# Products without use in TensorE's pauses: a one-core attention and expert kernel

## Chip, core and metric

The kernel runs on one core of one Trainium2 chip. The metric is the device time of one launch in microseconds (us). The kernel before takes 1171.12 us, the median of three runs (1170.22 to 1174.72). About half a per cent, some 5.9 us, is what a measurement of this kernel can tell from no change.

## What is computed

Four sublayers follow each other, each with a layer norm ahead of it, and a layer norm and an addition to x behind it:

```python
x = L0_attn_x                                              # (4, 512, 256)
x = x + _layernorm(_L0_attn_ref(_layernorm(x, axis=-1), ...), axis=-1)
x = x + _layernorm(_L0_ffn_ref(_layernorm(x, axis=-1), ...), axis=-1)
x = x + _layernorm(_L1_attn_ref(_layernorm(x, axis=-1), ...), axis=-1)
x = x + _layernorm(_L1_ffn_ref(_layernorm(x, axis=-1), ...), axis=-1)
```

Attention 0 has an RMS norm, 16 heads of 16, rotary embedding, a causal softmax, an output projection and a residual. The first feed-forward layer sends each token to 2 of 8 experts (256 to 1024 to 256), with at most 640 slots per expert. Attention 1 is a plain causal attention with 16 heads. The last layer computes all of 8 small gated experts and a shared one for every token, and mixes them by top-2 weights.

## The kernel before

The program is a row of blocks, and every engine waits for all others between two of them: setup, a first norm, attention 0 (`attention_phase` with `rope`), the experts (`expert_phase`), attention 1 (`attention_phase` without `rope`), the dense experts (`dense_phase`). Within a block the engines run their own instruction lists in order and meet by semaphores.

An attention handles 4 batches of 512 tokens. Its steady part is a loop over 16 steps (batch and group of four heads) and 11 places in each: TensorE (PE) computes scores for the row maxima into three PSUM banks `ps_a`, scores again into `ps_b`, products with the values into `ps_pv`, and at fixed places one "fill" of the two `ps_m` banks (`fill`: transposes, projections, outputs, routing). Ahead of the loop stand the fills of `FIRST`: the transposes of batch 0 (`yt`), its projections (`pr`) and values (`v`). They wait for `y_first`, the four normalised rows that VectorE (DVE) writes, and for the weights (`weights_in`).

Behind the loop stand the fills of `FINAL`, in the order in which TensorE does them:

```python
final = [("ot", last, 0), ("ot", last, 1), ("out", last, 0), ("out", last, 1)]
...
    final += [("rk", 2, 0), ("rt", last, 0), ("rt", last, 1), ("lg", last, 0), ("rk", last, 0)]
```

The second line is of attention 0 alone. `ot` and `out` are the last batch's output (L884, L901). `rk` counts for each token how many earlier ones chose its expert (two small bf16 matmuls, L869 and L871); `rt` and `lg` are the router's transposes and logits (L884, L862). DVE works through its own list there: it takes `out`, computes the statistics, and then, ahead of the normalisation of the last batch, turns the ranks of batch 2 into slots:

```python
variance(0, b)
if rope:
    place(2)                 # waits for ("rk", 2, 0) of TensorE
for i in range(TPB):
    ln_normalise(b, i)
```

After that come `ln_add`, the statistics of x, `route_rows` (what the transposes `rt` of the last batch wait for), `choose_top`, `count`, and `place` of the last batch. GpSimd (POOL) scatters the rows of batch 2 and of batch 3 to the experts' slots (L535) and waits until all have landed; then the block ends, its semaphores are cleared (L269), and the expert block loads its first rows.

Of the kernel before, what the change touches and what calls it, by code (L numbers as in the profile page):

```python
# [17 lines left out]
P = 128  # L18
BATCH, SEQ, D = 4, 512, 256
# [8 lines left out]
STEPS = BATCH * GROUPS  # L28
# [113 lines left out]
MAXES, PROBS = 11, 10  # L142
# [6 lines left out]
def need(eng, sem, count):  # L149

    if count > 0:
        eng.wait_ge(sem, count)
# [22 lines left out]
def prob_at(T, s):  # L175

    t, k = (T - 1, s - LAG) if s >= LAG else (T - 2, s - LAG + MAXES)
    return (t, k) if 0 <= t < STEPS and k < PROBS else None
# [74 lines left out]
def attention_phase(nc, keep, w, layer, route, w1=None, wide=None):  # L253

    wide = wide or []
    rope = layer == 0
# [9 lines left out]
    ident, identb, mask_q, minus_half = keep["ident"], keep["identb"], keep["mask_q"], keep["minus_half"]  # L266
    FILL, FIRST, FINAL, FILLS_AT, DONE_AT = misc_plan(rope, Q_TILES)
    held_sems = []
    with ExitStack() as ctx:  # L269
# [3 lines left out]
        def psum(name, shape, dt=F32):  # L273
            return ctx.enter_context(nc.psum_tensor(f"a{layer}_{name}", shape, dt))

        def sem(name):
            held_sems.append(nc.alloc_semaphore(name=f"a{layer}_{name}"))
            return held_sems[-1]
# [26 lines left out]
        ps_a = [psum(f"ps_a{i}", [P, SEQ]) for i in range(A_BANKS)]  # L305
# [4 lines left out]
        weights_in, cleared_rows, ones_in = sem("weights_in"), sem("cleared_rows"), sem("ones_in")  # L310
# [7 lines left out]
        a_full, a_free, b_full, exps = sem("a_full"), sem("a_free"), sem("b_full"), sem("exps")  # L318
# [49 lines left out]
        def emptied(eng, name):  # L368
            eng.wait_ge(m_free[FILL[name][0]], FILL[name][1] + 1)
# [412 lines left out]
        def _(pe):  # L782
# [4 lines left out]
            def max_unit(t, k):  # L787

                n = t * MAXES + k
                ps = ps_a[n % A_BANKS]  # L790
                need(pe, a_free, n - A_BANKS + 1)
                for h, i, at in max_work(k):
                    wd = (i + 1) * P
                    last = nc.tensor.matmul(ps[:, at:at + wd], q_st[t % STACKS][:, h // PER_TILE, i * P:wd],  # L794
                                            k_st[t % STACKS][:, h, 0:wd], start=True, stop=(k < 8),
                                            skip_group_check=True)
                    if k >= 8:
                        last = mask(ps, at + i * P)
                last.then_inc(a_full, 1)

            def prob_unit(t, k):

                n = t * PROBS + k
                ps = ps_b[n % B_BANKS]
                need(pe, exps, n - B_BANKS + 1)
                if k == 0 or (k == 2 and Q_TILES == 2):
                    emptied(pe, ("nm", t, k // 2))
                for h, j, at in prob_work(k):
                    wd = SEQ - j * P
                    last = nc.tensor.matmul(ps[:, at:at + wd], k_st[t % STACKS][:, h, j * P:(j + 1) * P],  # L810
                                            q_less[:, h // PER_TILE, j * P:SEQ], start=True, stop=True,
                                            skip_group_check=True)
                last.then_inc(b_full, 1)
# [14 lines left out]
            def pv(t, j):  # L828
                b, g = divmod(t, GROUPS)
                for h in range(HPG):  # L830
                    at = j * P
                    rhs = {0: probs[:, h, :], 1: probs[:, 4 + h, 0:3 * P], 3: probs[:, 4 + h, 3 * P:SEQ],
                           2: probs[:, 8 + h // 2, (h % 2) * 2 * P:(h % 2) * 2 * P + 2 * P]}[j]
                    last = nc.tensor.matmul(ps_pv[h * VW:(h + 1) * VW, at:SEQ], v[:, b % 2, j, g * HPG + h, :], rhs,  # L834
                                            start=(j == 0), stop=(j == 2), skip_group_check=True)
                return last
# [68 lines left out]
                    if half == 1:  # L905
                        last.then_inc(full, 1)

            pe.wait_ge(weights_in, 16 * (10 if rope else 3))
            def fill_whole(name):
                fill(name, 0)  # L910
                if name[0] in HALVED:
                    fill(name, 1)

            for name in FIRST:
                fill_whole(name)
            pe.wait_ge(identr_ready, 1)
            for T in range(STEPS + 2):
                for s in range(MAXES):
                    if T < STEPS:
                        if s == 0:  # L920
                            if T < STACKS:
                                pe.wait_ge(ones_in, (T + 1) * HPG)
                            pe.wait_ge(stacked[T % STACKS], 16 * 2 * HPG * (T // STACKS + 1))
                        max_unit(T, s)
                    if prob_at(T, s):
                        prob_unit(*prob_at(T, s))
                    for name, half in FILLS_AT.get((T, s), ()):
                        fill(name, half)
                    if s == 2 and 0 <= T - 2 < STEPS:
                        pe.wait_ge(masked, (T - 2) * 4 + 3)  # L930
                        pv(T - 2, 1)
                        pv(T - 2, 3).then_inc(pv_done, 1)
                    if s == 5 and 0 <= T - 2 < STEPS:
                        pe.wait_ge(masked, (T - 2) * 4 + 4)
                        pv(T - 2, 2).then_inc(pv_done, 1)
                    if s == 9 and 0 <= T - 1 < STEPS:
                        if (T - 1) % GROUPS == 0:
                            emptied(pe, ("v", (T - 1) // GROUPS, 0))
                            emptied(pe, ("v", (T - 1) // GROUPS, 1))
                        pe.wait_ge(masked, (T - 1) * 4 + 1)  # L940
                        need(pe, pv_copied, T - 1)
                        pv(T - 1, 0).then_inc(pv_done, 1)
            for name in FINAL:
                fill_whole(name)

        @block.vector
        def _(dve):
# [1122 lines left out]
def program(nc, io, out):  # L2070
    with ExitStack() as ctx:
        keep = keep_all(nc, ctx)
        scratch = [nc.dram_tensor(f"scratch{i}", (2, n, 3, P, SEQ), F32, kind="Internal").ap() for i, n in enumerate((2, 4))]
        dispatched = nc.dram_tensor("dispatched", ((E0 + 1) * CAP, D), F32, kind="Internal").ap()
        results = nc.dram_tensor("results", (SLOTS, D), F32, kind="Internal").ap()
        keep["cleared"] = ctx.enter_context(nc.semaphore("cleared"))
        keep["x_loaded"] = [ctx.enter_context(nc.semaphore(f"x_loaded{b}")) for b in range(BATCH)]
        setup_phase(nc, keep, io["x"])
        norm_phase(nc, keep)
        route = {"gates": ctx.enter_context(nc.sbuf_tensor("gates", [P, 2, TILES], F32)),  # L2080
                 "get_at": ctx.enter_context(nc.sbuf_tensor("get_at", [P, 2, TILES], U32))}
        with ExitStack() as moe:
            w1 = {part: moe.enter_context(nc.sbuf_tensor(f"w1_{part}", [P, KC, FF], F32 if part == "raw" else F32R))
                  for part in ("raw", "hi", "lo")}
            experts = {n[3:]: a for n, a in io.items() if n.startswith("m0_")} | {"dispatched": dispatched,
                                                                                 "results": results}
            attention_phase(nc, keep, {n[3:]: a for n, a in io.items() if n.startswith("a0_")} | experts
                            | {"scratch": scratch[0]}, 0, route, w1)
            w2 = {part: moe.enter_context(nc.sbuf_tensor(f"w2_{part}", [P, FC, D], F32 if part == "raw" else F32R))
                  for part in ("raw", "hi", "lo")}  # L2090
            expert_phase(nc, keep, experts, w1, w2)

        wide = [(io[f"m1_{n}"], *(ctx.enter_context(nc.sbuf_tensor(f"w_{n}_{part}", [P, KC, HB * H1], F32R))
                                  for part in ("hi", "lo"))) for n in ("gate", "up")]
        attention_phase(nc, keep, {n[3:]: a for n, a in io.items() if n.startswith("a1_")}
                        | {"scratch": scratch[1], "results": results}, 1, route, None, wide)
        dense_phase(nc, keep, {n[3:]: a for n, a in io.items() if n.startswith("m1_")}, wide, out)
# [41 lines left out]
```

## Time and profile before

| what | value |
|---|---|
| time, median of 3 runs | 1171.12 us (1170.22 to 1174.72) |
| time of the profiled execution | 1182.48 us |
| its span, first to last instruction | 1179.3 us |
| mean granted TensorE clock | 0.906 of full speed |
| PE busy | 975.2 us (83%) |
| DVE, POOL, ACT busy | 620.9, 464.2, 446.0 us |

The profiled execution is 11.4 us longer than the median of the others, and 3.2 us of it lie outside the span. PE is TensorE's matmuls, PEld its weight loads, ACT is ScalarE, SP the engine that issues most DMAs. PEclk is the share of full clock that TensorE was granted: 1.00 is 2.4 GHz and 0.50 is 1.2 GHz. Blocks lie in the span roughly so: attention 0 from 10 to 338 us, experts from 342 to 608, attention 1 from 608 to 952, dense experts from 956 to the end.

### The profile page before, as it was taken

What the parts mean: (1) busy time and instruction counts of PE and PEld (TensorE: products, weight loads), DVE (VectorE), ACT (ScalarE), POOL (GpSimd) and SP (SyncE); (2) the same over time, 40 slices, a digit from 0 to 9 for tenths busy, and PEclk for the clock granted to TensorE, in tenths of its full rate; (3) what the DMA queues carried; (4) which work ended last, traced back from release to release, by engine and by line L of the source; (5) the groups of instructions that cost most, each with busy time, mean ns of one, the idle gap of its engine ahead of it and who ended that gap; (6) DMA issues with size and microseconds to landing.
All of it is one profiled execution on the core that took longest, in us unless ns stands there. A gap on an engine that the chain in (4) does not pass through costs nothing. (4 is left out here: it accounts for less than half of the span.)

```text
span 1179.3 us, 17823 instructions
## 1 busy us (share of the span) xinstructions
PE 975.2 (83%) x6250; PEld 773.6 (66%) x6250; DVE 620.9 (53%) x1802; ACT 446.0 (38%) x800; POOL 464.2 (39%) x432
## 2 busy tenths in 40 slices
PE   3699999887419999999943489899999739999996
PEld 1466767564319999999941256575666427888885
DVE  5666787956513333333335767776666143353534
ACT  0155555443003333333300045555556314433332
POOL 3453544464523333222345243454243415434232
PEclk9799999897659999999985689999999659999998
DMA  3442212010142323332022552423310010000001
GB/s 129 160 149 95 81 54 92 26 50 10 63 173 95 112 90 111 116 115 94 22 83 69 187 170 77 160 87 112 126 55 28 1 46 1 1 2 18 18 1 36
DMA packets 50023, 91.78 MB, mean 78 GB/s; under 512 B 7328, under 2 KB 22944, under 8 KB 49824
## 3 DMA queue, kind: packets, MB, share of 16 engines
q1 hardware_dynamic: 46880, 82.49, 20.8%
q0 software_dynamic: 3072, 8.39, 2.2%
q8 instruction: 39, 0.64, 0.2%
q14 instruction: 32, 0.26, 0.1%
HBM read 54.55 MB, written 36.31 MB: 77 GB/s over the span
## 5 line engine op out<-in xcount | busy, mean ns | idle before, releaser
L746 ACT ACTIVATE a_probs<-a_ps_b 128x512 f32<-128x512 f32 x320 | 188.1, 600 | 190.2 <-PE a_ps_b L810 186.4
L794 PE MATMUL a_ps_a<-a_k_st,a_q_st 128*128 128x256 f32 (+3 forms) x512 | 204.2, 440 | 26.9 <-DMA a_k_st<-scratch 17.3
L1004 DVE CUSTOM_DVE_ANT_0 a_masked_s<-a_ps_a,a_mask_f 128x512 f32<-128x512 f32 (+1 forms) x256 | 155.2, 621 | 86.6 <-PE a_ps_a L794 80.6
L794 PEld LDWEIGHTS a_ps_a<-a_k_st,a_q_st 128*128 128x128 f32 x512 | 102.5, 203 | 89.6 <-issue 42.6
L475 POOL TENSOR_SCALAR_AFFINE_SELECT a_probs<-a_probs 128x512 f32<-128x512 f32 x128 | 80.9, 646 | 198.3 <-ACT a_probs L746 198.0
L1594 POOL TENSOR_TENSOR w_lo<-w_raw,w_hi 128x2048 fp32r<-128x2048 f32 x16 | 73.9, 4616 | 186.7 <-ACT w_hi L1612 186.7
L810 PE MATMUL a_ps_b<-a_q_less,a_k_st 128*128 128x384 f32 (+3 forms) x512 | 140.2, 337 | 3.0 <-ACT a_probs L746 2.1
L810 PEld LDWEIGHTS a_ps_b<-a_q_less,a_k_st 128*128 128x128 f32 x512 | 91.3, 197 | 28.6 <-ACT a_probs L746 17.8
L1620 ACT ACTIVATE exp_h_hi<-exp_ps_u 128x320 fp32r<-128x320 f32 x128 | 49.2, 437 | 148.4 <-PE exp_ps_u L1684 148.4
L834 PE MATMUL a_ps_pv<-a_probs,a_v 128*32 128x512 f32 (+3 forms) x1024 | 94.9, 470 | 10.7 <-POOL a_probs L475 10.7
L1649 DVE SCALAR_TENSOR_TENSOR exp_h_lo<-exp_ps_u,exp_h_hi 128x320 fp32r<-128x320 f32 x128 | 56.8, 485 | 69.5 <-ACT exp_h_hi L1620 69.5
L1799 POOL TENSOR_TENSOR dense_h_lo<-dense_mixed,dense_h_hi 128x512 fp32r<-128x512 f32 x40 | 52.1, 1303 | 104.1 <-ACT dense_h_hi L1852 104.1
L1699 PE MATMUL exp_ps_o<-w_hi,exp_h_hi 128*128 128x256 f32 x320 | 91.2, 285 | 0.0
L1699 PE MATMUL exp_ps_o<-w_hi,exp_h_lo 128*128 128x256 f32 x320 | 90.5, 283 | 0.0
L1699 PE MATMUL exp_ps_o<-w_lo,exp_h_hi 128*128 128x256 f32 x320 | 90.5, 283 | 0.0
L1011 DVE TENSOR_REDUCE a_nmax<-a_ps_a 128x2 f32<-128x512 f32 (+1 forms) x96 | 65.9, 687 | 40.5 <-PE a_ps_a L784 38.4
L884 PE MATMUL a_ps_m<-kept_ident,kept_sub 128*128 128x128 f32 x160 | 30.5, 333 | 65.2 <-DVE kept_sub L950 33.9
L2038 DVE TENSOR_TENSOR dense_product<-dense_gated,dense_ps_u 128x512 f32<-128x512 f32 x40 | 27.5, 687 | 87.1 <-PE dense_ps_u L1869 81.3
L891 PE MATMUL a_ps_m<-a_y_t,a_w_qk 128*128 128x512 f32 x128 | 69.6, 645 | 3.0 <-ACT a_y_t L648 1.9
L884 PEld LDWEIGHTS a_ps_m<-kept_ident,kept_sub 128*128 128x128 f32 x160 | 24.4, 175 | 68.6 <-issue 48.4
L1659 DVE COPY exp_out<-exp_ps_o 128x512 f32<-128x512 f32 (+1 forms) x24 | 14.5, 603 | 97.9 <-PE exp_ps_o L1699 97.9
L1684 PE MATMUL exp_ps_u<-exp_x_t_hi,w_hi 128*128 128x320 f32 x256 | 60.3, 317 | 3.1 <-DVE exp_h_lo L1649 1.9
(238 smaller groups left out, 2296.2 us busy)
## 6 DMA issues: line engine op xcount, KB each, us to landing
w_raw<-in_m_w SPq DMA_DIRECT2D x16, 1024.0 KB, 5.1
scratch<-a_hi SPq DMA_DIRECT2D x24, 512.0 KB, 2.8
scratch<-a_lo SPq DMA_DIRECT2D x24, 256.0 KB, 3.1
a_q_st<-scratch SPq DMA_DIRECT2D x64, 96.0 KB, 2.6
a_k_st<-scratch SPq DMA_DIRECT2D x64, 96.0 KB, 2.6
exp_rows<-dispatched SPq DMA_DIRECT2D x9, 640.0 KB, 4.2
results<-exp_out SPq DMA_DIRECT2D x8, 640.0 KB, 3.0
dispatched<-kept_sub SPq DMA_DIRECT2D x9, 512.0 KB, 2.9
```

Source lines behind the costliest of these rows:

```text
L475: nc.gpsimd.affine_select(out=blocks, in_=blocks, compare_op=ALU.is_ge, fill=0.0, base=0, pattern=[[0, HPG], [1, P]], channel_multiplier=- ...
L746: nc.scalar.activation(probs[:, k, :], ps_b[k % B_BANKS][:, :], ACT.Exp, scale=scale).then_inc(exps, 1)
L794: last = nc.tensor.matmul(ps[:, at:at + wd], q_st[t % STACKS][:, h // PER_TILE, i * P:wd], k_st[t % STACKS][:, h, 0:wd], start=True, stop= ...
L810: last = nc.tensor.matmul(ps[:, at:at + wd], k_st[t % STACKS][:, h, j * P:(j + 1) * P], q_less[:, h // PER_TILE, j * P:SEQ], start=True, s ...
L834: last = nc.tensor.matmul(ps_pv[h * VW:(h + 1) * VW, at:SEQ], v[:, b % 2, j, g * HPG + h, :], rhs, start=(j == 0), stop=(j == 2), skip_gro ...
L891: last = nc.tensor.matmul(ps[:, :], w_qk[:, half, n, :], y_t[:, half, :], start=(half == 0), stop=(half == 1))
L1004: nc.vector.tensor_tensor_reduce(masked_s[n % 2][:, 0:wd], ps[:, 0:wd], mask_f[:, SEQ - wd:SEQ], -1.0, -NEG, ALU.add, ALU.min, nmax[:, t % ...
L1011: nc.vector.tensor_reduce(out, src, AX_X, ALU.max, negate=True).then_inc(a_free, 1)
L1594: nc.gpsimd.tensor_tensor(of["lo"][:, :, :], of["raw"][:, :, :], of["hi"][:, :, :].bitcast(F32), ALU.subtract).then_inc(ready, 1)
L1649: nc.vector.scalar_tensor_tensor(h[1][:, f, cols], ps_u[n % U_BANKS][:, 0:HALF], 0.0, h[0][:, f, cols].bitcast(F32), ALU.max, ALU.subtract ...
L1684: last = nc.tensor.matmul(ps_u[(2 * f + half) % U_BANKS][:, 0:HALF], (w1["hi"], w1["lo"])[i][:, c, f * P:(f + 1) * P], x_t[j][:, c * CAP + ...
L1699: last = nc.tensor.matmul(bank[:, t % 2 * D:(t % 2 + 1) * D], h[i][:, f, t * P:(t + 1) * P], (w2["hi"], w2["lo"])[j][:, f, :], start=(f == ...
```

## The change

TensorE is given products that nothing reads. Each multiplies the bf16 identity by itself, repeated to 512 columns, into the bank `ps_a[0]`. There are 12 ahead of the first transposes of attention 0 and 90 ahead of those of attention 1, both ahead of TensorE's wait for the weights; 36 behind the last `out` fill of each attention; and 60 behind the last `rk` fill of attention 0. Ahead of `FINAL` a wait for the last of DVE's row maxima is added, since the products overwrite a bank that they read. In all 12 + 36 + 60 + 90 + 36 = 234 products.

```diff
-            pe.wait_ge(weights_in, 16 * (10 if rope else 3))
             def fill_whole(name):
                 fill(name, 0)
                 if name[0] in HALVED:
                     fill(name, 1)
 
+            def idle_products(count):
+
+                for _ in range(count):
+                    nc.tensor.matmul(ps_a[0][:, :], identb[:, :], identb[:, :].unsqueeze(1).to_broadcast([P, SEQ // P, P]),
+                                     start=True, stop=True, skip_group_check=True)
+
+            idle_products(12 if rope else 90)
+            pe.wait_ge(weights_in, 16 * (10 if rope else 3))
             for name in FIRST:
                 fill_whole(name)
...
+            pe.wait_ge(a_free, STEPS * MAXES)
             for name in FINAL:
                 fill_whole(name)
+                if name == ("out", BATCH - 1, 1):
+                    idle_products(36)
+                if name == ("rk", BATCH - 1, 0):
+                    idle_products(60)
```

TensorE's instructions at the end of attention 0 in the kernel before, from the last batch's output transposes (L884) to the block's end (L269); `a_hot_sum` and `a_prior` are the operands of an `rk` fill:

```order
L884 MATMUL a_ps_m<-kept_ident,kept_sub 128x128 x8
L901 MATMUL a_ps_m<-a_w_o,a_o_t 128x256 x8
L869 MATMUL a_ps_m<-a_hot_sum,a_before 128x32
L871 MATMUL a_ps_m<-a_prior,a_ones 128x32
L884 MATMUL a_ps_m<-kept_ident,kept_sub 128x128 x8
L862 MATMUL a_ps_m<-a_w_g,a_ry_t 128x8 x8
L869 MATMUL a_ps_m<-a_hot_sum,a_before 128x32
L871 MATMUL a_ps_m<-a_prior,a_ones 128x32
L269 UNCONDITIONAL_BRANCH
```

The same place in the changed kernel:

```order
L884 MATMUL a_ps_m<-kept_ident,kept_sub 128x128 x8
L901 MATMUL a_ps_m<-a_w_o,a_o_t 128x256 x8
L916 MATMUL a_ps_a<-kept_identb 128x512 x36
L869 MATMUL a_ps_m<-a_hot_sum,a_before 128x32
L871 MATMUL a_ps_m<-a_prior,a_ones 128x32
L884 MATMUL a_ps_m<-kept_ident,kept_sub 128x128 x8
L862 MATMUL a_ps_m<-a_w_g,a_ry_t 128x8 x8
L869 MATMUL a_ps_m<-a_hot_sum,a_before 128x32
L871 MATMUL a_ps_m<-a_prior,a_ones 128x32
L916 MATMUL a_ps_a<-kept_identb 128x512 x60
L269 UNCONDITIONAL_BRANCH
```

The numbers at a row's end count matmuls as the program issues them; in the trace an f32 matmul that is not a transpose shows as two instructions. The 36 stand between the last `out` and the ranks of batch 2, so these two small matmuls are moved behind them; the 60 stand between the last ranks and the end of the block. At the start of each attention the products are the block's first instructions on TensorE.

## Rows read from the trace of the kernel before

**Rows 1.** The page's part 2: granted clock, 40 equal slices of the span.

```profile
PEclk9799999897659999999985689999999659999998
```

**Rows 2.** Timeline, TensorE, end of attention 0: start, duration, what, idle before.

```profile
297.40 5.56 PE L901 MATMUL a_ps_m<-a_w_o,a_o_t 128*128 128x256 f32 x16 [0.87 <-ACT a_o_t L685]
302.80 0.18 PE L869 MATMUL a_ps_m<-a_hot_sum,a_before 128*128 128x32 bf16 x1
314.27 1.94 PE L884 MATMUL a_ps_m<-kept_ident,kept_sub 128*128 128x128 f32 x8 [11.27 <-DVE kept_sub L1089]
323.80 0.19 PE L871 MATMUL a_ps_m<-a_prior,a_ones 128*128 128x32 bf16 x1
346.17 1.97 PE L1672 MATMUL exp_ps_t<-kept_ident,exp_rows 128*128 128x128 f32 x8 [22.18 <-DMA exp_rows<-dispatched]
```

**Rows 3.** Timeline, VectorE and GpSimd, end of attention 0.

```profile
305.00 0.28 DVE L1141 TENSOR_TENSOR a_picked<-a_hot,a_ps_m 128x32 f32<-128x32 f32 x2
...
335.32 0.97 POOL L535 DMA_INDIRECT dispatched<-kept_sub,a_put_at  x1 [0.30 <-issue]
```

**Rows 4.** Windows: length, busy time of each engine, granted clock, DMA.

```profile
303.10:308.00 4.90, 0.00 (x0) 0.00 (x0) 4.47 (x21) 0.00 (x0) 1.04 (x1) 1.00 0.00 0
308.10:314.20 6.10, 0.00 (x0) 0.00 (x0) 5.71 (x22) 0.00 (x0) 2.23 (x3) 0.50 0.00 0
314.20:324.00 9.80, 5.71 (x26) 5.19 (x26) 2.69 (x23) 1.41 (x3) 6.62 (x7) 0.50 0.30 108
346.20:355.80 9.60, 7.85 (x30) 7.05 (x30) 2.69 (x5) 2.31 (x5) 0.00 (x0) 0.50 0.80 308
```

**Rows 5.** Windows behind the last scatter of attention 0, same columns.

```profile
337.00:337.50 0.50, 0.00 (x0) 0.00 (x0) 0.00 (x0) 0.00 (x0) 0.00 (x0) 0.50 0.40 139
337.50:338.00 0.50, 0.00 (x0) 0.00 (x0) 0.00 (x0) 0.00 (x0) 0.00 (x0) 0.50 0.00 0
```

**Rows 6.** Timeline, TensorE, dense block: 512-column matmuls before and after the clock rises.

```profile
972.34 0.63 PE L1869 MATMUL dense_ps_g<-dense_y_t_hi,w_gate_lo 128*128 128x512 f32 x1
972.77 0.63 PE L1869 MATMUL dense_ps_u<-dense_y_t_hi,w_up_hi 128*128 128x512 f32 x1
...
974.08 0.40 PE L1869 MATMUL dense_ps_u<-dense_y_t_lo,w_up_hi 128*128 128x512 f32 x1
974.32 0.40 PE L1869 MATMUL dense_ps_u<-dense_y_t_hi,w_up_lo 128*128 128x512 f32 x1
```

**Rows 7.** Weight loads by shape: count, busy us, mean ns, idle before.

```profile
L784 PEld LDWEIGHTS a_ps_a<-kept_mask_q,kept_identb 128*128 128x128 bf16 x256 | 25.7, 101 | 8.1 <-issue 2.1
...
L1869 PEld LDWEIGHTS dense_ps_g<-dense_y_t_lo,w_gate_hi 128*128 128x128 f32 x80 | 15.6, 196 | 2.0
```

**Rows 8.** Timeline, start of attention 0, columns as in Rows 2.

```profile
10.55 1.38 DVE L950 TENSOR_SCALAR kept_sub<-kept_x,kept_mean,kept_rin 128x256 f32<-128x256 f32 x4 [0.54 <-PEq L1411]
...
17.61 1.97 PE L884 MATMUL a_ps_m<-kept_ident,kept_sub 128*128 128x128 f32 x8 [17.61 <-DMA a_w_g<-in_m_g]
...
26.29 1.65 DVE L976 SCALAR_TENSOR_TENSOR a_part_q<-a_ps_m,a_bias,a_rot 128x512 f32<-128x512 f32 x2
```

**Rows 9.** Timeline, start of attention 1.

```profile
608.68 1.76 DVE L1252 MEMSET a_k_st<- 128x2048 f32 x1 [4.02 <-PEq L1502]
...
640.79 9.66 PE L891 MATMUL a_ps_m<-a_y_t,a_w_qk 128*128 128x512 f32 x16 [0.77 <-ACT a_y_t L650]
```

**Rows 10.** Windows, start of attention 1, columns as in Rows 4.

```profile
638.00:645.90 7.90, 7.05 (x14) 3.75 (x15) 0.69 (x1) 1.76 (x3) 0.00 (x0) 0.50 0.00 0
```

**Rows 11.** Timeline, end of attention 1.

```profile
936.70 6.75 PE L901 MATMUL a_ps_m<-a_w_o,a_o_t 128*128 128x256 f32 x16 [0.77 <-ACT a_o_t L688]
...
951.44 1.01 POOL L502 TENSOR_TENSOR kept_rstd<-a_var_eps,kept_minus_half 128x4 f32<-128x4 f32 x1 [4.88 <-DVE a_var_eps L1064]
```

**Rows 12.** Windows, start of the dense block, columns as in Rows 4.

```profile
946.40:959.80 13.40, 0.00 (x0) 0.00 (x0) 8.13 (x20) 0.00 (x0) 3.87 (x5) 0.50 0.15 43
959.80:973.60 13.80, 10.88 (x40) 9.36 (x41) 3.57 (x23) 3.05 (x5) 0.00 (x0) 0.50 0.14 56
```

## Prediction, made before the changed kernel ran

> **What bounds the kernel now.** I read the page's clock line first [rows 1]. Its digits fall to 5 or 6 in three stretches (about 290 to 354, 619 to 678 and 914 to 973 us), where blocks meet, and to 7 at the very start; elsewhere it is mostly full. A change that only gives TensorE work in its pauses can win time there alone: by a higher clock for the matmuls behind the pause. So each pause was looked up in the timeline and in windows, with three questions: how long is it, who ends it, and who waits for TensorE inside it.
>
> At the end of attention 0 the pauses are not one but four. TensorE does the outputs from 297.40, the ranks of batch 2 at 302.80, then waits for the last batch's rows until 314.27, does the ranks of batch 3 at 323.80, and waits for the experts' rows until 346.17 [rows 2]. The chain through this stretch is VectorE's, not TensorE's. But VectorE's list contains `place(2)`, which needs the ranks of batch 2: it starts at 305.00, two microseconds after the ranks are there [rows 3]. That is all the slack these two small matmuls have. Everything that ends the stretch stands behind it: the normalisation of batch 3, its rows, its logits, its ranks, and the scatter whose last piece GpSimd issues at 335.32 [rows 3].
>
> At the starts the first transposes wait for a DMA (17.61) in attention 0 [rows 8] and for VectorE's rows in attention 1 and in the dense block. There TensorE is free from 608.7 to 638.0 [rows 9, 10] and from 943.45 to 959.8 (936.70 + 6.75, then the idle window) [rows 11, 12].
>
> **What one product costs.** No row shows a bf16 product of 512 columns. The nearest are f32 ones of 512 columns, each with its own weight load: 0.43 us from start to start at clock 0.5 (972.34 to 972.77) and 0.23 to 0.24 us at full clock (974.08 to 974.32) [rows 6]. Their weight loads of 196 ns [rows 7] do not show as extra time. bf16 may lack the small excess over half of 0.43, so the warm price lies between 0.215 and 0.233; I take 0.22, and 0.43 cold. What the cold stretch at the start of such work costs is also taken from rows: attention 1's projections start at 640.79 and run at 0.50 to 645.9, 5.2 us with rounding [rows 9, 10]. I take 5.2, with nothing and one microsecond more (6.2) as ends.
>
> **12 products at the start of attention 0.** TensorE enters about 10.3 us (VectorE starts there at 10.55), so 12 x 0.43 = 5.2 us end at 15.5, ahead of the DMA at 17.61 [rows 8]. Cost nothing. If they raise the clock, transposes and the first projections end earlier, but VectorE takes these only at 26.29, when its own fills of memory are done, with no idle time noted before it [rows 8]. Gain nothing. That cover is VectorE's memsets; without it up to a microsecond or two could be won.
>
> **36 products behind the outputs of attention 0.** These stand between the outputs and the ranks of batch 2. By 303.1 the clock is full [rows 4], so they take 36 x 0.22 = 7.9 us and the ranks start at 302.80 + 7.9 = 310.7, ready 0.2 us later. VectorE would have read them at 305.00, so it is late by 310.9 - 305.0 = **5.9 us**, and the whole chain to the end of the block with it. With 0.215 it is 5.7, with 0.233 it is 6.4. What they could bring is a full clock for the transposes and logits of batch 3, which run at 0.50 now (5.7 us busy) [rows 4]. But TensorE then pauses from 311.0 to 314.27 + 5.9 = 320.2, 9.2 us. Before, a pause that began at 303.0 kept full clock to 308.0 and ran at half from 308.1 [rows 4]: 5 us is the longest pause with the clock up that these rows show. So that work stays cold. Gain nothing.
>
> **60 products behind the last ranks.** They start at 323.80 + 0.19 + 5.9 = 329.9 with a cold clock: 5.2 us are 12 products, 48 more at 0.22 are 10.6, end at 345.7. The block ends when the last scatter has landed: DMA traffic stops by 337.5 [rows 5], with the delay 343.4. So TensorE itself becomes the last to arrive, by **2.3 us** (none if the clock rises at once, 3.3 with 6.2 us cold and 0.233). The experts' first rows are loaded only after this, so TensorE pauses again from 345.7 to 346.17 + 8.2 = 354.4, 8.7 us: cold again, and nothing is won on the expert block's first matmuls (7.85 us busy at 0.50 [rows 4]).
>
> **90 products at the start of attention 1.** From 608.7: 5.2 us cold (12), 78 x 0.22 = 17.2, end at 631.1. The transposes come at 638.0: 6.9 us later. No delay, and most likely no warm clock.
>
> **36 products behind attention 1.** From 943.45, 7.9 us, end at 951.4. GpSimd's last root ends at 951.44 + 1.01 = 952.45 [rows 11], so they are just covered; without that cover each further microsecond is paid. The dense block's transposes come 8.4 us after them: cold again.
>
> The added wait for VectorE's row maxima is for work that ended two steps earlier: nothing.
>
> **Sum.** 5.9 + 2.3 = 8.2 us. On the profiled execution 1182.48 + 8.2 = 1190.7; that execution is 11.4 us above the median of the others, and nothing in the sum depends on that excess, so the median goes from 1171.1 to 1179.3 us, 0.7% slower. Its own range is 1176.8 (5.7 and no lateness) to 1180.8 (6.4 + 3.3).
>
> **A rule against the price of a product.** Rows 6 give 0.23 us and hide the weight load. The Trainium skill, page "TensorE: Matmul & The Clock Gate", "Back-to-back issue gap", gives a sustained spacing of about 131 ns per 512-column matmul in a real kernel. No spacing in rows 6 comes near it, so the trace disagrees. By it 36 products would take 4.7 us, the delay would be 2.7 us, and the 60 would be covered. The same page says under "What overlaps and what doesn't" that a weight load overlaps a running matmul only when the row group differs, which these do not; rows 6 and 7 disagree with that as well, for f32. A result of each stands among the rivals.
>
> **Rivals.**
> (a) The clock lasts through one pause, that ahead of attention 1, which is the shortest (6.9 us, 5.6 if the products are at the slow ends). Then half of the 7.05 us that TensorE works at 0.50 there [rows 10] is won, 3.5 us: 1175.8 us, within half a per cent. For it: 5.6 is near the 5 us seen. Chance 0.18.
> (b) Faster: the clock lasts through all pauses of 7 to 9.2 us. Then half of the cold work behind each is won: 7.85/2 + 10.88/2 + 7.05/2 + 5.7/2 = 15.7 us [rows 4, 10, 12], and the 60 products, warm from the start, take 13.2 us and are no longer late (2.3): 1179.3 - 18.0 = 1161.3. It decides from a holding time of about 9 us on. Against it: half clock 5 us into a pause [rows 4]. Chance 0.06.
> (c) Products are longer, because the identity's load isn't hidden: 0.10 us more each (bf16 loads are 101 ns [rows 7]), 0.32 warm and 0.53 cold. Then 9.5 us at the ranks, 7.8 us at the block's end, 1.5 us late in attention 1 but 3.5 won by the warm clock, 2.5 us late at its end: +17.8, 1188.9 us. Against it: rows 6. Chance 0.07.
> (d) The spacing is much shorter, 0.131: +2.7, 1173.8 us. No row supports it. Chance 0.03.
> (e) The change does not do what it says: such products do not raise the clock, and all run at 0.43. 36 take 15.5 us, 60 take 25.8, 90 take 38.7: 13.5 + 12.3 + 9.3 + 6.5 = +41.6, 1212.7 us. Dense f32 matmuls raise it in rows 6, so 0.03.
>
> **How the numbers follow.** My forecast has 0.55, the five rivals 0.37; 0.08 is left for what I don't see, such as the clock falling elsewhere by another phase, in either direction. Slower by over 0.5% (5.9 us, what a measurement can tell) is nearly all of the forecast, whose low end just falls short of it (0.52), with (c), (e) and half of the rest: 0.65. Within 0.5%: (a), (d) and some of both: 0.27. Faster: (b) and a little: 0.08. The range must reach to (a) and nearly to (c): 1173 to 1186.
>
> **What would show it.** In the profile of the changed kernel: `place(2)` on VectorE waits for the ranks some 5.9 us, right behind the statistics of the output; 36 products of 0.22 us stand ahead of them; the last of the 60 ends later than the last scatter's landing; the clock is at 0.50 again when the transposes of batch 3, of the experts, of attention 1 and of the dense block start. I am wrong if the clock is full in these places, if VectorE finds the ranks ready at `place(2)`, or if a product's spacing is far from 0.22.

## The result, and the profile after

The changed kernel takes 1182.53 us, the median of 20 runs (1172.72 to 1187.95), beside 1174.15 us for the kernel before on the same chip (20 runs, 1169.63 to 1181.99). The ratio is 1.0059, 95% interval 1.0037 to 1.0081: 0.6% slower, some 6.9 us. The profiled execution takes 1186.39 us with a span of 1184.7, 5.4 us more than that of before, at a mean granted clock of 0.921 instead of 0.906. TensorE's clock is higher and the kernel is slower. Of the changed kernel's 20 runs five, with a mean granted clock of 0.934 or 0.935, take 1172.7 to 1174.4 us; the other 15, at 0.918 to 0.928, take 1181.1 to 1188.0.

First the page's clock line and the row of the products in the groups of instructions (busy us, mean ns, idle before), beside [rows 1]:

```profile
PEclk8799999897779999999988689999999778999998
```

```profile
L916 PE MATMUL a_ps_a<-kept_identb 128*128 128x512 bf16 x234 | 58.7, 417 | 14.5 <-PEq L1423 10.4 <-PEq L1514 4.0
```

Then the timeline of TensorE at the start and where blocks meet, beside [rows 2, 8, 9, 11]:

```profile
10.42 4.58 PE L916 MATMUL a_ps_a<-kept_identb 128*128 128x512 bf16 x12 [10.42 <-PEq L1423]
17.56 1.97 PE L884 MATMUL a_ps_m<-kept_ident,kept_sub 128*128 128x128 f32 x8 [2.56 <-DMA a_w_g<-in_m_g]
...
297.15 5.53 PE L901 MATMUL a_ps_m<-a_w_o,a_o_t 128*128 128x256 f32 x16 [0.87 <-ACT a_o_t L685]
302.51 7.93 PE L916 MATMUL a_ps_a<-kept_identb 128*128 128x512 bf16 x36
310.31 0.18 PE L871 MATMUL a_ps_m<-a_prior,a_ones 128*128 128x32 bf16 x1
319.81 1.94 PE L884 MATMUL a_ps_m<-kept_ident,kept_sub 128*128 128x128 f32 x8 [9.33 <-DVE kept_sub L1101]
...
329.37 15.88 PE L916 MATMUL a_ps_a<-kept_identb 128*128 128x512 bf16 x60
351.60 1.97 PE L1684 MATMUL exp_ps_t<-kept_ident,exp_rows 128*128 128x128 f32 x8 [6.35 <-DMA exp_rows<-dispatched]
...
612.60 22.39 PE L916 MATMUL a_ps_a<-kept_identb 128*128 128x512 bf16 x90 [4.04 <-PEq L1514]
643.46 1.94 PE L884 MATMUL a_ps_m<-kept_ident,kept_sub 128*128 128x128 f32 x8 [8.47 <-DVE kept_sub L962]
646.16 8.53 PE L891 MATMUL a_ps_m<-a_y_t,a_w_qk 128*128 128x512 f32 x16 [0.77 <-ACT a_y_t L650]
...
947.98 7.93 PE L916 MATMUL a_ps_a<-kept_identb 128*128 128x512 bf16 x36
964.53 1.12 PE L1893 MATMUL dense_ps_t<-kept_ident,kept_sub 128*128 128x128 f32 x4 [8.61 <-DVE kept_sub L1981]
```

And VectorE, GpSimd and the queue of SP around the end of attention 0, beside [rows 3]:

```profile
304.64 0.17 DVE L1076 TENSOR_SCALAR a_var_eps<-a_moments 128x4 f32<-128x4 f32 x1
310.52 0.29 DVE L1153 TENSOR_TENSOR a_picked<-a_hot,a_ps_m 128x32 f32<-128x32 f32 x2 [5.71 <-PE a_ps_m L871]
...
340.88 0.97 POOL L535 DMA_INDIRECT dispatched<-kept_sub,a_put_at  x1 [0.30 <-issue]
...
347.38 0.36 SPq L1552 DMA_DIRECT2D exp_rows<-dispatched  x1
```

The windows, with columns as in [rows 4]:

```profile
319.80:329.30 9.50, 5.50 (x24) 5.05 (x25) 2.69 (x23) 1.41 (x3) 6.56 (x7) 0.50 0.32 113
351.60:358.90 7.30, 5.55 (x21) 4.76 (x22) 1.81 (x3) 1.54 (x3) 0.00 (x0) 0.50 1.03 401
638.80:649.00 10.20, 4.78 (x12) 2.89 (x13) 4.51 (x4) 1.17 (x2) 3.40 (x2) 0.50 0.01 3
959.70:980.10 20.40, 12.68 (x45) 10.75 (x46) 7.08 (x27) 4.81 (x8) 4.13 (x5) 0.50 0.19 66
```

What is to be seen: between `a_var_eps` and `a_picked` (`place(2)`) VectorE is idle for 5.71 us and waits for L871 on TensorE. In [rows 3] no idle time stands there. On TensorE 36 products stand ahead of L871, from 302.51 to 310.28. The start of `place(2)` moves from 0.08 to 5.88 us behind `a_var_eps`, by 5.8 us, where the spans differ by 5.4: this one wait accounts for the slowdown of this pair of traces. The longer rows of products do bring the clock to full (90 take 22.39 us, where 0.43 us each would make 38.7), but where they stand the idle time ahead of the next work is still 9.33, 6.35, 8.47 and 8.61 us, and the windows of that work read 0.50 again, as they did before.

For all comparisons below the span was cut at the same events in each trace. The numbers are differences of start times in the timelines, in us. "Wait" is from the start of `a_var_eps` to that of `place(2)`; "routing" from `place(2)` to the ranks of batch 3 on VectorE (the start of `a_rank`); "experts" from their first load to the first load of attention 1; "rows" from that load to the first transposes; "start" from there to the first scores; "loop 1" from there to the dense block's first load; "dense" from there to the end; "loop 0" from attention 0's first scores to its last outputs.

| kernel | loop 0 | wait | routing | experts | rows | start | loop 1 | dense |
|---|---|---|---|---|---|---|---|---|
| before | 254.1 | 0.08 | 19.34 | 266.4 | 29.9 | 25.5 | 292.7 | 223.0 |
| changed | 254.0 | 5.88 | 19.37 | 265.2 | 30.9 | 24.9 | 292.6 | 223.7 |
| e1 | 250.3 | 0.08 | 17.70 | 265.2 | 29.9 | 25.2 | 293.1 | 222.4 |
| e2 | 251.5 | 5.02 | 19.37 | 265.7 | 30.9 | 25.2 | 291.1 | 223.1 |
| e3 | 255.8 | 5.89 | 19.36 | 265.8 | 30.9 | 25.2 | 291.2 | 223.1 |
| e4 | 250.7 | 2.62 | 19.36 | 265.2 | 30.3 | 22.6 | 291.0 | 219.7 |
| e5 | 249.7 | 0.08 | 18.26 | 264.3 | 29.9 | 25.4 | 292.5 | 218.1 |
| e6 | 250.0 | 0.08 | 18.25 | 264.3 | 29.9 | 23.9 | 289.5 | 219.6 |
| e7 | 250.1 | 3.38 | 19.37 | 265.5 | 30.9 | 25.0 | 292.9 | 223.8 |
| e8 | 255.7 | 13.66 | 19.36 | 266.5 | 29.9 | 25.5 | 292.9 | 223.0 |
| e9 | 254.2 | 0.08 | 19.36 | 266.4 | 29.9 | 25.5 | 292.7 | 219.5 |
| e10 | 250.4 | 0.08 | 18.59 | 263.2 | 29.9 | 24.8 | 292.9 | 223.8 |

Changed against before: +5.8 for the wait, -1.2 in the experts, +1.0 in the rows, -0.6 at the start of attention 1, -0.1 and +0.7 behind it. The added wait for the row maxima shows nowhere: no idle time stands ahead of the last output transposes of attention 0 (294.58 before, 294.33 after), and 0.90 us stand ahead of those of attention 1 in both, put down to their rows.

### The profile page after: what moved, and what is told of

The parts are those of the page before. It is cut to its first block and busy times, and to the rows that moved or that the text cites. A ratio compares the mean times of both kernels' runs of the same rounds, so it can differ in the third digit from the quotient of the medians.

```text
span 1184.7 us, 18293 instructions
## 1 busy us (share of the span) xinstructions
PE 1031.9 (87%) x6484; PEld 797.1 (67%) x6484; DVE 620.5 (52%) x1802; ACT 446.0 (38%) x800; POOL 464.7 (39%) x432
## 5 line engine op out<-in xcount | busy, mean ns | idle before, releaser
L916 PE MATMUL a_ps_a<-kept_identb 128*128 128x512 bf16 x234 | 58.7, 417 | 14.5 <-PEq L1423 10.4
L1711 PEld LDWEIGHTS exp_ps_o<-w_hi,exp_h_hi 128*128 128x128 f32 x320 | 61.4, 192 | 0.3
```

The costliest lines, as they stand in the source:

```text
L1711: last = nc.tensor.matmul(bank[:, t % 2 * D:(t % 2 + 1) * D], h[i][:, f, t * P:(t + 1) * P], (w2["hi"], w2["lo"])[j][:, f, :], start=(f == ...
```

## Experiments

Each is an edit of the changed kernel, e9 and e10 of the kernel before. Runs e1 to e4, e5 to e8, and e9 with e10 each shared a chip. The kernel before had medians of 1183.14, 1180.14 and 1178.6 us on these, so each time is to be read by its ratio. The theories, in words: the 36 products cost their own length less a slack, by their place in TensorE's queue ahead of the ranks; the 60 make the block end late, or something else ends it and they are free; and a pause brings a warm clock only if it is filled up to the next work.

**e1_ranks_first.** The 36 products of attention 0 stand behind the ranks of batch 2.

```diff
-                if name == ("out", BATCH - 1, 1):
+                if name == (("rk", 2, 0) if rope else ("out", BATCH - 1, 1)):
                     idle_products(36)
```

> The changed kernel, but in attention 0 the 36 products stand behind the ranks of batch 2 instead of ahead of them. Theory S (the slowdown is VectorE's wait for these ranks): VectorE finds them ready at place(2), the wait of 5.7 us is gone, the gap from the statistics of the output to the experts' first loads is as in the kernel before (341.82 - 304.92 = 36.9 us), and the time is 5.5 us under the changed kernel's, within half a per cent of the kernel before. Rival C (the slowdown comes from the clock falling elsewhere, or from the products beside other work): the wait goes but the time stays some 6 us or more over the kernel before.

Measured: 1181.22 us (10 runs), ratio 0.9980 (0.9965 to 0.9995). Timelines of TensorE and of VectorE:

```profile
300.59 0.19 PE L871 MATMUL a_ps_m<-a_prior,a_ones 128*128 128x32 bf16 x1
300.62 10.76 PE L916 MATMUL a_ps_a<-kept_identb 128*128 128x512 bf16 x36
312.46 1.07 PE L884 MATMUL a_ps_m<-kept_ident,kept_sub 128*128 128x128 f32 x8 [1.08 <-DVE kept_sub L1101]
...
303.10 0.17 DVE L1076 TENSOR_SCALAR a_var_eps<-a_moments 128x4 f32<-128x4 f32 x1
303.18 0.28 DVE L1153 TENSOR_TENSOR a_picked<-a_hot,a_ps_m 128x32 f32<-128x32 f32 x2
```

The ranks come at 300.6, ahead of the products, and `place(2)` starts 0.08 us behind `a_var_eps`. The loss is gone by this one move of two small matmuls, and rival C, by which the time would stay, is out. The pause ahead of the transposes is 1.08 us instead of 9.33, their eight take 1.07 us instead of 1.94, and "routing" is 1.6 us shorter. From the ranks of batch 3 to the last scatter are 11.80 us instead of 10.98, so half of that is lost again. VectorE and GpSimd:

```profile
322.31 0.17 DVE L1162 TENSOR_SCALAR a_far<-a_fits 128x8 f32<-128x8 f32 x1 [0.86 <-DVE a_fits L1161]
323.74 0.97 POOL L535 DMA_INDIRECT dispatched<-kept_sub,a_put_at  x1 [2.90 <-DVEq L1165]
```

VectorE stands still for 0.86 us on its way to the slots, and GpSimd, idle for 2.90 us, waits for these. No run shows why; e5, e6 and e10 gained in "routing" and have the 10.98 to 11.00 us of all others.

**e2_without_60.** No products behind the last ranks.

```diff
-                if name == ("rk", BATCH - 1, 0):
-                    idle_products(60)
```

> The changed kernel without the 60 products at the end of attention 0. Theory L (my prediction's second term: TensorE arrives last at the block's end): from the last scatter's issue to the experts' first load it is shorter than the changed kernel's by up to 2.3 us. Rival N (the 60 are covered by the landing and by the clearing of the semaphores behind it): that distance is 6.5 us as in both traces so far (341.82 - 335.32, 347.38 - 340.88), and the time is the changed kernel's within its scatter, some 6 to 8 us over the kernel before.

Measured: 1186.01 us (12 runs), ratio 1.0028 (1.0011 to 1.0045). From the last scatter to the experts' first load are 6.50 us with the 60 and without them (338.90 to 345.40 here, 340.88 to 347.38 in the changed kernel), as in all twelve traces. They are free, and my term for them was wrong. The median is 3.3 us over that of the kernel before and not 6 to 8 as expected; the wait in this trace is 5.02 us.

**e3_only_36.** Of the whole change only the 36 products of attention 0 are left.

```diff
-            idle_products(12 if rope else 90)
...
-                if name == ("out", BATCH - 1, 1):
+                if rope and name == ("out", BATCH - 1, 1):
                     idle_products(36)
-                if name == ("rk", BATCH - 1, 0):
-                    idle_products(60)
```

> The kernel before with nothing but the 36 products ahead of the ranks in attention 0. Theory S: +5.5 us, all of it in VectorE's wait at place(2), and the ratio is about 1.005. Rival C: the other 198 products carry the slowdown and this kernel is within 2 us of the kernel before in spite of the wait.

Measured: 1188.06 us (12 runs), ratio 1.0031 (1.0013 to 1.0049), with a wait of 5.89 us at `place(2)`. The wait is the same as with all 234 products. The intervals of e1 and e3 don't meet. In the median the 36 cost 3.7 us, somewhat less than the 1.005 expected and than the wait of this one trace.

**e4_fill_125.** 125 instead of 90 products ahead of attention 1, so that they reach its transposes.

```diff
-            idle_products(12 if rope else 90)
+            idle_products(12 if rope else 125)
```

> The changed kernel with 125 products instead of 90 at the start of attention 1, so that they end about 642.4 instead of 634.9, a microsecond ahead of the transposes at 643.5. Theory H (the clock is lost in the 8.5 us between the 90 and the transposes; what decides is how long TensorE has been idle): transposes and projections run at full clock, the stretch from the first transpose to the last projection takes 3 to 4 us less (before: 638.08 to 650.45, 12.4 us), and the time is 3 us under the changed kernel's. Rival P (the pace there is set by ScalarE's and VectorE's work on the banks, not by the clock): the clock is full and the stretch is less than 1 us shorter.

Measured: 1183.54 us (12 runs), ratio 1.0001 (0.9983 to 1.0018). Timeline of TensorE:

```profile
633.25 5.35 PE L916 MATMUL a_ps_a<-kept_identb 128*128 128x512 bf16 x24 [0.28 <-issue]
638.44 1.04 PE L884 MATMUL a_ps_m<-kept_ident,kept_sub 128*128 128x128 f32 x8
640.36 7.11 PE L891 MATMUL a_ps_m<-a_y_t,a_w_qk 128*128 128x512 f32 x16 [0.88 <-ACT a_y_t L650]
```

There is no pause left; the transposes take 1.04 us instead of 1.94 and the projections 7.11 instead of 8.53 (9.66 in [rows 9]), and the first scores come 22.6 us behind the transposes. In the traces with 90 products and a gap they come 24.9 to 25.5 us behind them, and in those without any products there (before, e3, e9, e10) 24.8 to 25.5: with the gap open the 90 bring nothing that can be told, and 35 more that close it bring 2.2 to 2.9 us. The ratio of the medians does not show this alone, since the wait at `place(2)` is only 2.62 us in this trace.

**e5_fill_all.** All pauses filled to their ends, and the 36 behind the ranks. Into the experts' and the dense block's own lists go 18 + 6 and 15 + 6 + 6 products of the same kind.

```diff
-            idle_products(12 if rope else 90)
+            idle_products(0 if rope else 122)
             pe.wait_ge(weights_in, 16 * (10 if rope else 3))
             for name in FIRST:
                 fill_whole(name)
+            idle_products(40 if rope else 36)
...
-                if name == ("out", BATCH - 1, 1):
-                    idle_products(36)
+                if name == (("rk", 2, 0) if rope else ("out", BATCH - 1, 1)):
+                    idle_products(44 if rope else 50)
```

> Products without use in every pause, none ahead of the ranks of batch 2, and none ahead of the first transposes: 44 behind these ranks, 60 at the block's end, 18 at the start of the expert block and 6 behind its first transposes, 122 at the start of attention 1, 50 at its end, 15 at the start of the dense block and 6 behind each of its two first fills of transposes, and 40 and 36 between the first values and the loop of the two attentions. Theory H (the clock was lost in the 5 to 9 us that the changed kernel's numbers leave open; work behind a pause is set by TensorE's clock): full clock at these places, half of the cold work is won, about 1.5 us in the routing, 3 to 4 at the experts' start, 3 in attention 1, 5 in the dense block, and up to 4 at each loop's start: 12 to 20 us under the kernel before, ratio 0.983 to 0.990. Rival P (others set the pace there): the clock is full and each stage is less than a microsecond shorter, ratio above 0.995.

Measured: 1171.33 us (12 runs), ratio 0.9951 (0.9925 to 0.9977). Timeline of TensorE:

```profile
310.51 1.06 PE L884 MATMUL a_ps_m<-kept_ident,kept_sub 128*128 128x128 f32 x8 [2.31 <-DVE kept_sub L1102]
...
336.87 5.61 PE L1722 MATMUL exp_ps_u<-kept_identb 128*128 128x512 bf16 x18 [2.81 <-PEq L1388]
342.32 1.04 PE L1685 MATMUL exp_ps_t<-kept_ident,exp_rows 128*128 128x128 f32 x8
...
631.13 1.06 PE L884 MATMUL a_ps_m<-kept_ident,kept_sub 128*128 128x128 f32 x8 [0.89 <-DVE kept_sub L963]
...
935.99 10.96 PE L916 MATMUL a_ps_a<-kept_identb 128*128 128x512 bf16 x50
949.00 3.40 PE L1971 MATMUL dense_ps_d<-kept_identb 128*128 128x512 bf16 x15 [2.06 <-PEq L1388]
952.54 0.66 PE L1903 MATMUL dense_ps_t<-kept_ident,kept_sub 128*128 128x128 f32 x4
...
956.85 0.25 PE L1891 MATMUL dense_ps_t<-dense_w_r_lo,dense_y_t_hi 128*128 128x10 f32 x1
956.96 0.25 PE L1891 MATMUL dense_ps_t<-dense_w_r_hi,dense_y_t_lo 128*128 128x10 f32 x1
```

The transposes of all four places run at full clock, and the dense block's small score matmuls follow each other at 0.11 us (956.85 to 956.96). "Dense" is 4.9 us shorter, "experts" 2.1, "routing" 1.1. But "start" is 25.4, hardly less than before. The projections in the timeline of TensorE:

```profile
633.08 8.80 PE L891 MATMUL a_ps_m<-a_y_t,a_w_qk 128*128 128x512 f32 x16 [0.88 <-ACT a_y_t L650]
```

The granted clock is 0.81 on average in these 8.80 us: behind the transposes it was at half again for a while, with pauses of only 0.89 and 0.88 us before. In e4 the projections ran at 1.00 and took 7.11 us. The whole kernel gains half a per cent. Theory H had forecast 12 to 20 us (0.983 to 0.990), which is missed; the stages gain more than the microsecond of rival P, all but "start", and the ratio of 0.9951 is just within what rival P allowed.

**e6_fill_meetings.** As e5 without the products between the first values and the loops.

```diff
-            idle_products(40 if rope else 36)
```

> As the one that fills every pause, but with nothing between the first values and the loop of each attention. Theory H: both loops start cold again and this is 3 to 8 us over that kernel. Rival D (at the loops' start VectorE's maxima and the loads of the next stacks set the pace): within 2 us of it.

Measured: 1172.2 us (12 runs), ratio 0.9948 (0.9924 to 0.9973). Timeline of TensorE:

```profile
655.68 1.62 PE L794 MATMUL a_ps_a<-a_k_st,a_q_st 128*128 128x512 f32 x3 [8.28 <-DMA a_k_st<-scratch]
663.82 3.37 PE L794 MATMUL a_ps_a<-a_k_st,a_q_st 128*128 128x512 f32 x6 [6.52 <-DVE a_nmax L1016]
```

Nothing is lost without those 76 products, as rival D said: the start of this loop waits 8.28 us for loads and then 6.52 us for VectorE's row maxima. This kernel and e5 beat both the kernel before, by about half a per cent, and the changed one.

**e7_changed_again.** The changed kernel itself, on the chip of e5, e6 and e8.

> The changed kernel once more, for the comparison on one chip: the ratio to the kernel before is again 1.003 to 1.008, and in the profile VectorE waits 5.7 us at place(2). If the scatter of its times comes from where the clock falls, its stages that differ from the first profile are those in which TensorE runs at another clock.

Measured: 1182.99 us (12 runs), ratio 1.0045 (1.0018 to 1.0072). The wait at `place(2)` is only 3.38 us here. Timelines of TensorE and VectorE:

```profile
293.71 3.69 PE L901 MATMUL a_ps_m<-a_w_o,a_o_t 128*128 128x256 f32 x16 [1.00 <-ACT a_o_t L685]
297.24 7.93 PE L916 MATMUL a_ps_a<-kept_identb 128*128 128x512 bf16 x36
...
299.94 0.69 DVE L1059 TENSOR_TENSOR kept_sub<-a_ps_m,a_resid 128x512 f32<-128x512 f32 x1 [1.41 <-remote]
305.25 0.28 DVE L1153 TENSOR_TENSOR a_picked<-a_hot,a_ps_m 128x32 f32<-128x32 f32 x2 [3.21 <-PE a_ps_m L871]
```

In this execution the outputs ran at full clock, 3.69 us instead of 5.53, and VectorE waited 1.41 us in between for something that the profile does not name. TensorE was ahead by more, so the same 36 products cost less; a wait of 5.7 us had been expected again. 36 products are 7.8 us; less the 5.8 that the wait grew by, the slack was 2.0 us in the first trace, as in [rows 2, 3], and less 3.3 it is 4.5 here.

**e8_double.** 72 instead of 36 products in attention 0.

```diff
-                    idle_products(36)
+                    idle_products(72 if rope else 36)
```

> The changed kernel with 72 products instead of 36 ahead of the ranks in attention 0. Theory S: VectorE's wait at place(2) grows by 36 x 0.216 = 7.8 us, from 5.7 to 13.5, and from there to the experts' first load nothing changes (36.9 us from place(2)). Rival C: the wait grows, but the stretch behind it gets shorter because the clock is still full at the router's transposes (9.3 us after the products in the changed kernel, the same here), by 2 us or more.

Measured: 1197.72 us, a single run, so there is no ratio. The wait is 13.66 us, 7.8 more than with 36, and 36 x 0.216 = 7.8. The rest of the stretch stays as it was. Past the slack each product costs its full length, and rival C, a shorter stretch behind it, is out.

**e9_dense_only.** The kernel before, with products only between attention 1 and the dense block (and the wait for the row maxima, which they need).

```diff
                 fill_whole(name)
+                if name == (("rk", 2, 0) if rope else ("out", BATCH - 1, 1)):
+                    idle_products(0 if rope else 50)
...
+            idle_products(15)
...
+                idle_products(6)
```

> The kernel before with products in one pause alone, that between attention 1 and the dense block, but without a gap: 50 behind the last outputs of attention 1, 15 at the start of the dense block, 6 behind each of its first two groups of transposes. Theory H (a pause pays for what stands behind it, if it is filled to its end, and each place by itself): from the dense block's first transposes to the end 219.5 becomes some 214.5 us, all other stretches stay as before, and the time falls by 5 us, a ratio of 0.996. 
Measured: 1176.65 us (12 runs), ratio 0.9970 (0.9938 to 1.0002). Timeline of TensorE:

```profile
943.44 10.95 PE L916 MATMUL a_ps_a<-kept_identb 128*128 128x512 bf16 x50
956.45 5.08 PE L1966 MATMUL dense_ps_d<-kept_identb 128*128 128x512 bf16 x15 [2.06 <-PEq L1385]
961.38 0.60 PE L1898 MATMUL dense_ps_t<-kept_ident,kept_sub 128*128 128x128 f32 x4
```

From the transposes to the end are 214.5 us, what theory H gave. But 1.4 us of that are paid ahead of it: the 15 products began partly cold, took 5.08 us instead of 3.40 (e5), and the transposes, 3.6 us behind the first load in all other traces, came 5.0 us behind it. The net gain in the trace is 3.5 us. All other stretches are those of before within 0.3 us, so nothing was taken back in it. But the interval reaches 1, so the medians alone do not exclude rival P, and the gain rests on this pair of traces.

**e10_experts_only.** The kernel before, with products only around the end of attention 0.

```diff
                 fill_whole(name)
+                if name == (("rk", 2, 0) if rope else ("out", BATCH - 1, 1)):
+                    idle_products(44 if rope else 0)
+                if name == ("rk", BATCH - 1, 0):
+                    idle_products(60)
...
+            idle_products(18)
...
+            idle_products(6)
```

> The kernel before with products in the pauses around the end of attention 0 alone: 44 behind the ranks of batch 2 (not ahead of them), 60 behind those of batch 3, 18 at the start of the expert block, 6 behind its first transposes. Theory H: from the ranks of batch 2 to those of batch 3 on VectorE 19.3 becomes 18.3 us; from the experts' first transposes to the end of their block 262.0 becomes some 259 us; attention 1 and the dense block stay as before; some 4 us less in all, a ratio of 0.9965. No wait of VectorE at place(2). Rival P: under 1 us in all, a ratio of 1.000, with what is won at the experts' start given back within their block, whose pace GpSimd and the loads would set.

Measured: 1172.77 us (12 runs), ratio 0.9956 (0.9927 to 0.9984). Timeline of TensorE:

```profile
297.93 9.66 PE L916 MATMUL a_ps_a<-kept_identb 128*128 128x512 bf16 x44
309.37 1.06 PE L884 MATMUL a_ps_m<-kept_ident,kept_sub 128*128 128x128 f32 x8 [1.78 <-DVE kept_sub L1101]
...
336.07 4.04 PE L1721 MATMUL exp_ps_u<-kept_identb 128*128 128x512 bf16 x18 [3.45 <-PEq L1387]
340.31 1.09 PE L1684 MATMUL exp_ps_t<-kept_ident,exp_rows 128*128 128x128 f32 x8 [0.20 <-DMA exp_rows<-dispatched]
```

"Experts" is 3.2 us shorter and "routing" 0.75; from the experts' first transposes to the end of their block are 259.0 us instead of 262.0, as theory H gave. The rest of its trace, chiefly loop 0, is luck: the code up to there is that of before, and e6 and e9, whose code is the same there, show 250.0 and 254.2. The median of 12 runs is 5.8 us lower, more than the 3.9 of these two stretches, but its interval (1.9 to 8.6 us) holds both.

## Why the prediction was right, and where not

**The forecast.** 1.0070 was predicted (1179.3 over 1171.12) and 1.0059 (1.0037 to 1.0081) measured. The time itself, 1182.5 us, lies in the range, 3 us above the forecast, and the kernel before was 3.0 us slower too on the chip that compared them.

**One product.** 36 products from 302.51 to 310.28 are 0.216 us each. I took 0.22, within 0.215 and 0.233. Each has its weight load of 105 ns, which adds nothing, so rival (c) is out, and so is the 0.131 of rival (d): this is a stream of 36 with nothing between, and 0.216 is all that it gives. The Trainium skill, page "TensorE: Matmul & The Clock Gate", "What overlaps and what doesn't", lets a load overlap only where the row group differs. This trace disagrees for bf16 as well: all rows of the array (128*128) are used by each, and 0.216 us leave no room for the load. With (e), that such products don't raise the clock, the 90 would have taken 38.7 us; they took 22.4.

**12 products: right.** They end at 15.0, and the transposes wait for the DMA until 17.56 (17.61 before).

**36 ahead of the ranks: right, with too narrow a range.** Predicted +5.9 us in the profiled execution, measured 5.8. e1, e3 and e8 show the cause: taken behind the ranks, alone, and doubled, the wait goes to 0.08, stays at 5.89, and grows by the length of the added products. But I treated the slack of 2.0 us as a constant. It was 4.5 in e7, where the outputs ran at full clock, so the cost is 3.3 us there, and only 2.5 in e4's trace. The low end of 5.7 was too high. How often the smaller cost occurs is not known: the medians of e2 and e3 are 3.3 and 3.7 us over the kernel before, but their intervals reach to 5.3 and 5.8.

**60 behind the last ranks: wrong.** The step that failed is "the block ends when the last scatter has landed: DMA traffic stops by 337.5". The products ended where I put them (345.25, forecast 345.7), but the block doesn't end with the traffic: the experts' first load comes 6.50 to 6.51 us after the start of the last scatter in every trace, with or without the 60. In the changed kernel the last DMA packet ends 4.44 us ahead of that load and TensorE 2.13 us ahead of it: TensorE is 2.3 us behind the traffic, as forecast, and delays nothing. What fills the 4.4 us, no run shows. The row for it stood in the trace: in the kernel before TensorE had been idle since 324.0, and still the load did not come before 341.8. The term measures 0 instead of 2.3.

**90 and 36 in attention 1: right.** 22.39 us for the 90 (5.2 + 17.2 = 22.4 predicted), pauses of 8.47 and 8.61 us behind them (6.9 and 8.4 predicted), 0.50 at both transposes. The pause that rival (a) was about came out longer than its 6.9 us; but the shortest, 6.35 us ahead of the experts, also ends at 0.50. So rivals (a) and (b) are out. The second half of (b), that a warm clock pays for what stands behind it, is right once the pause is gone, though less than I priced: I gave 15.7 us for all four. e5 and e6 show 8.2 us each in "routing", "experts", "start" and "dense" together, and some 6 us in the medians. In e5 and e6 the clock fell again behind the first transposes of attention 1, and not all of the cold work need have been on the path, which no run separates. These sums are rough: "dense" is 219.7 us in e4, whose start there is cold, and 219.6 in e6, whose start is filled. For the dense block e9 is the cleaner evidence, since the rest of its trace is that of before.

**The sum.** 8.2 us predicted, 5.4 in the pair of traces and some 6.9 in the medians. In the traces the missing lateness of the 60 takes 2.3 off and two small gains ("experts", "start") 1.8 more, and 1.7 come on top in "rows" and "dense". All four lie within what single traces differ by, or nearly: without the 90 products "start" is 24.8 in e10 and 25.2 in e3, without the 60 "experts" is 265.7 and 265.8 in e2 and e3, and "dense" is 219.7 to 223.8 in the traces where its start is cold. What is not settled: "rows" is 1.0 us longer in the changed kernel, e2, e3 and e7, but not in e1 and e8; e3 has no products there and the others have the same 90. Where it is longer one of GpSimd's gathers takes 1.93 instead of 1.01 us. It has no tie to an edit that I can show.

## What to carry to other kernels

Work that is put into an idle engine costs its length less the slack of the first instruction behind it in that engine's queue, even where the engine is mostly waiting: ask of each instruction that is passed who reads its result, and when. Put such products behind the last small matmul that somebody waits for, not ahead of it. Products for the clock's sake pay only if they reach the work that they are meant for; here gaps of 6 to 10 us left open gave back nothing that can be told from chance, and closed, or nearly, they gave about 1 us in the routing, 2 to 3 us in the experts, up to 2.9 us at the start of attention 1 and 3.5 us net in the dense block. That is half a per cent of the kernel in all.

## What the runs showed of the hardware that was not expected

The clock's falls come at other places from run to run. "Loop 0" took 249.7 to 255.8 us in these traces, though its code is the same but for products at its start, and the changed kernel's own 20 runs span 15 us. In the longer traces of 254 to 256 us, and in e2 (251.5), the outputs at its end ran partly at half clock (5.53 us for 16 matmuls in the changed kernel's, at 0.66 on average), in that of e7 and the other short ones at full (3.69). The total times of one trace each are therefore not a comparison of two kernels. Stretches cut at the same events show where the time goes, but those that hang on the clock differ by 4 to 6 us without an edit ("dense", "loop 0"), while "wait" is 0.08 us in all traces without products ahead of the ranks. In "loop 1" two differences cancel: in the changed kernel the last outputs of attention 1 start 1.5 us later after the first scores than before, and take 5.19 us instead of 6.75.
